# Spreading attention queries over edges as three bf16 parts instead of float32, in a graph kernel on one core

## What is computed

```python
q = (h @ Wq.T + bq)[dst]; k = (h @ Wk.T + bk)[src]; v = (h @ Wv.T + bv)[src]   # 8 heads of 16
alpha = jnp.sum(q * k, axis=-1) / 4
ex = jnp.exp(alpha - segment_max(alpha, dst)[dst])
out = segment_sum(ex / segment_sum(ex, dst)[dst] * v, dst)
x_r = h @ Ws.T + bs; h = gate(out, x_r) ...; layer norm; feed-forward          # 4 layers
msg = silu([x[src], x[dst], rbf(edge_len)] @ mw1 + mb1) @ mw2 + mb2             # message layer
agg = segment_sum(msg, dst) / count
```

## Time and profile before

| | |
|---|---|
| median of 3 runs | 7938.27 us (7920.73 to 7941.61) |
| the profiled execution's own time | 7866.28 us |
| its span in the trace | 7864.5 us |
| mean granted clock of TensorE | 0.685 of full |
| busy: PE, PEld, VectorE | 4591.8, 3687.8, 4054.1 us |
| busy: ScalarE, POOL | 2762.9, 3848.5 us |

### The profile page before, as it was taken

One profiled execution on the slowest core, in us unless ns is written; L12 is line 12 of the kernel. 1 busy time (PEld: TensorE's weight loads), 2 busy tenths in 40 slices (PEclk: granted clock), 3 DMA queues, 4 the chain that ended last, 5 costly groups with the idle time before them and its releaser, 6 DMA issues.

```text
span 7864.5 us, 105863 instructions
## 1 busy us (share of the span) xinstructions
PE 4591.8 (58%) x22799; PEld 3687.8 (47%) x22800; DVE 4054.1 (52%) x11127; ACT 2762.9 (35%) x6393; POOL 3848.5 (49%) x4061
## 2 busy tenths in 40 slices
PE   4555555655555556555555565555555655666666
PEld 2444444534444445344444453444444544555555
DVE  4555555645555556455555564555555653333334
ACT  1333333423333334233333342333333432333333
POOL 3555555335555553345555543455555425555553
PEclk6666666676666666766666667666666677878788
DMA  4222222122222222222222222222222211111111
GB/s 127 78 78 74 78 78 77 52 66 76 78 77 79 76 79 57 65 69 77 77 79 77 79 61 68 68 78 78 78 76 80 60 31 44 44 45 45 45 44 27
DMA packets 267185, 536.12 MB, mean 68 GB/s; under 512 B 116251, under 2 KB 148687, under 8 KB 266507
## 3 DMA queue, kind: packets, MB, share of 16 engines
q0 software_dynamic: 180992, 490.24, 23.2%
q1 hardware_dynamic: 78899, 35.89, 1.8%
q10 hardware_dynamic: 6936, 6.69, 0.3%
HBM read 512.41 MB, written 18.03 MB: 67 GB/s over the span
## 4 chain that ended last, share of the span: by engine, by line
PE 27%; another core or an unknown queue 25%; issue 20%; DVE 17%; ACT 5%; DVEq 4%; ACTq 1%; DMA 0%; SPq 0%; POOL 0%; POOLq 0%
PE bank L765 9%; PE bank L784 8%; DVE acc L1191 6%; PE bank L769 2%; PE bank L756 2%; ACT oh L549 2%; DVEq L330 2%; PE bank L805 2%; PE bank L833 1%; DVE alpha L1214 1%; DVEq L1191 1%; DVE slots L1283 1%; DVE oh L1175 1%; PE bank L937 1%
## 5 line engine op out<-in xcount | busy, mean ns | idle before, releaser
L504 POOL DMA_INDIRECT slots<-kv_table,idx x3224 | 3065.0, 951 | 3149.1 <-PE bank L784 1272.7
L784 PE MATMUL bank<-slots,oh 128*128 128x136 f32 (+1 forms) x8060 | 1598.6, 352 | 584.7 <-DVE acc L1191 502.7
L765 PE MATMUL bank<-qs,ohT 128*128 x8080 | 1676.3, 354 | 230.3 <-ACT ohT L540 132.0
L784 PEld LDWEIGHTS bank<-slots,oh 128*128 128x128 f32 x8060 | 1415.4, 253 | 716.9 <-DVE acc L1191 614.8
L765 PEld LDWEIGHTS bank<-qs,ohT 128*128 128x128 f32 x8080 | 1428.7, 256 | 450.4 <-issue 428.3
L1191 DVE TENSOR_TENSOR acc<-acc,bank 128x136 f32 (+1 forms) x4030 | 1173.6, 291 | 603.7 <-PE bank L784 166.4
L1208 DVE TENSOR_TENSOR slots<-slots,bank 128x512 f32<-128x512 f32 x808 | 552.3, 684 | 1312.1 <-remote 1294.4
L540 ACT ACTIVATE ohT<-bank,miss 128x512 f32<-128x512 f32 x1010 | 676.5, 683 | 1360.0 <-PE bank L756 1226.6
L504 POOL DMA_INDIRECT slots<-src_table,idx x806 | 760.8, 944 | 750.5 <-DMA idx<-src_e 233.6
L549 ACT ACTIVATE oh<-iota,rel_e 128x128 f32<-128x128 f32 x3168 | 962.9, 387 | 0.0
L797 PE MATMUL bank<-ident,alpha 128*128 128x128 f32 x204 | 93.7, 459 | 1459.5 <-DVE alpha L1214 1423.0
(11 more groups left out here) (255 smaller groups left out, 4032.7 us busy)
## 6 DMA issues: line engine op xcount, KB each, us to landing
slots<-kv_table,idx POOLq DMA_INDIRECT x3224
kv_table<-slots SPq DMA_DIRECT2D x20, 660.0 KB, 3.4
slots<-src_table,idx POOLq DMA_INDIRECT x806
resets<-flat_len ACTq DMA_DIRECT2D x51, 128.0 KB
idx<-src_e SPq DMA_DIRECT2D x255, 8.0 KB
terms<-flat_rel SPq DMA_DIRECT2D x255, 12.0 KB
resets<-flat_rst SPq DMA_DIRECT2D x2, 1551.0 KB
w<-in_w SPq DMA_DIRECT2D x8, 256.0 KB
```

Source lines behind the costliest of these rows:

```text
L504: pool.indirect_dma_start(slots[:, k, t, 0:width], None, table, bass.IndirectOffsetOnAxis(ap=idx[:, k, t:t + 1], axis=0))\
L765: mm = pe.matmul(o, ohT[:, j % 2, t, :], qs[:, blocks[j * G + t], 0:HID], start=True, stop=basis is None)
L784: mm = pe.matmul(bank[6 + part % 2][:, o:o + width], oh[:, k % 2, t, :], slots[:, k, t, HID:HID + width], start=True, stop=True)
```

## The change

Queries (and the destinations' part in the message pass) are kept as three bf16 numbers whose sum is their float32 value: the first two in the place in `qs` where the float32 value stood (`q_pair`), the third in a new tile `q_low`. `ohT` becomes bf16. Line 765 becomes three bf16 matmuls that add into the same PSUM place. VectorE makes the parts five blocks at a time (`in_parts`: a copy to bf16, a difference, a copy, a difference, over 5 x 128 columns). At a layer's start a block is therefore taken in two instructions, the query half into a float32 place in `oh`, the skip half into `qs`. A new semaphore `parts_done` holds PE back from the first spreading of a layer. The memory that software-made transfers use for their descriptors is set to 8192 bytes of a partition.

```diff
+        q_low = sb("q_low", [P, NB, HID], BF16)
+        q_pair = qs[:, :, :].bitcast(BF16)
-        ohT = sb("ohT", [P, 2, G, P])
+        ohT = sb("ohT", [P, 2, G, P], BF16)
+        whole = oh[:, 1, BW:2 * BW, :]
...
-                    mm = pe.matmul(o, ohT[:, j % 2, t, :], qs[:, blocks[j * G + t], 0:HID],
-                                   start=True, stop=basis is None)
+                    b = blocks[j * G + t]
+                    pe.matmul(o, ohT[:, j % 2, t, :], q_pair[:, b, 0:HID], start=True, stop=False)
+                    pe.matmul(o, ohT[:, j % 2, t, :], q_pair[:, b, HID:2 * HID], start=False, stop=False)
+                    mm = pe.matmul(o, ohT[:, j % 2, t, :], q_low[:, b, :], start=False, stop=basis is None)
...
+                pe.wait_ge(parts_done, START + NI * (l + 1))
...
+            pe.wait_ge(parts_done, START + NI * (L + 1))
...
+            def in_parts(first, end, rest, step):
+
+                step(dve.tensor_copy(q_pair[:, first:end, 0:HID], rest))
+                step(dve.tensor_tensor(rest, rest, q_pair[:, first:end, 0:HID], ALU.subtract))
+                step(dve.tensor_copy(q_pair[:, first:end, HID:2 * HID], rest))
+                return dve.tensor_tensor(q_low[:, first:end, :], rest, q_pair[:, first:end, HID:2 * HID], ALU.subtract)
...
-                    dve.tensor_tensor(qs[:, b, :], bank[6 + b % 2][:, 0:QS], vec_qs[:, :], ALU.add).then_inc(q_ev, 1)
+                    if b % BW == 0 and b > 0:
+                        dve.wait_ge(parts_done, START + NI * l + b // BW)
+                    dve.tensor_tensor(whole[:, b % BW, :], bank[6 + b % 2][:, 0:HID], vec_qs[:, 0:HID], ALU.add)
+                    dve.tensor_tensor(qs[:, b, HID:QS], bank[6 + b % 2][:, HID:QS], vec_qs[:, HID:QS], ALU.add).then_inc(q_ev, 1)
+                    if b % BW == BW - 1:
+                        dve.wait_ge(q_ev, START + NB * l + b + 1)
+                        in_parts(b - BW + 1, b + 1, whole, step).then_inc(parts_done, 1)
...
-                dve.tensor_tensor(qs[:, i * BW:i * BW + 4, 0:HID], bank[7][:, :].rearrange("p (b k) -> p b k", b=4),
+                dve.tensor_tensor(o_c[i][:, 0:4, :], bank[7][:, :].rearrange("p (b k) -> p b k", b=4),
                                   bc(bias, 4), ALU.add).then_inc(pair_q, 1)
-                dve.tensor_tensor(qs[:, i * BW + 4, 0:HID], bank[4][:, 0:HID], bias, ALU.add).then_inc(pair_q, 1)
+                dve.tensor_tensor(o_c[i][:, 4, :], bank[4][:, 0:HID], bias, ALU.add).then_inc(pair_q, 1)
+                dve.wait_ge(pair_q, START + 2 * i + 2)
+                in_parts(i * BW, (i + 1) * BW, o_c[i], step).then_inc(parts_done, 1)
...
-    nc = bacc.Bacc("TRN2", target_bir_lowering=False, num_devices=1)
+    nc = bacc.Bacc("TRN2", target_bir_lowering=False, num_devices=1, dynamic_dma_scratch_size=8192)
```

More of the change, by code:

```diff
@@ L270, in build_program @@
         rcol_done, fwd_one, bwd_one = sem("rcol_done"), sem("fwd_one"), sem("bwd_one")
+        parts_done = sem("parts_done")
         rows_turned, rows_copied, carry_set = sem("rows_turned"), sem("rows_copied"), sem("carry_set")
@@ L280, in build_program @@
         out_ready, out_sent = sem("out_ready"), sem("out_sent")
-        counted = [sums_ready, deviations_ready, x_sums, x_devs, in_ps, in_act, s_ps, q_ev, h_ev, f2_ps, wo_ps, wo_ev, x_new, x_ps, x_out, src_ps, dst_ps, r_ps, pair_q, pair_s, a_ev, a_ps, acc_done, part_ps, acc_scaled, acc_zero, act_ans, act_req,
+        counted = [parts_done, sums_ready, deviations_ready, x_sums, x_devs, in_ps, in_act, s_ps, q_ev, h_ev, f2_ps, wo_ps, wo_ev, x_new, x_ps, x_out, src_ps, dst_ps, r_ps, pair_q, pair_s, a_ev, a_ps, acc_done, part_ps, acc_scaled, acc_zero, act_ans, act_req,
                    alpha_done, alpha_turned, arg_done, b_done, bwd_one, bwd_two, carries_packed,
@@ L1467, in new_x, with destinations @@
                 dve.wait_ge(x_new, START + i + 1)
-            def destinations(i):
+            def destinations(i, step):
                 bias = vec1[:, VEC1["mb1"]:VEC1["mb1"] + HID]
                 dve.wait_ge(dst_ps, START + i + 1)
-                dve.tensor_tensor(qs[:, i * BW:i * BW + 4, 0:HID], bank[7][:, :].rearrange("p (b k) -> p b k", b=4),
+                dve.tensor_tensor(o_c[i][:, 0:4, :], bank[7][:, :].rearrange("p (b k) -> p b k", b=4),
                                   bc(bias, 4), ALU.add).then_inc(pair_q, 1)
-                dve.tensor_tensor(qs[:, i * BW + 4, 0:HID], bank[4][:, 0:HID], bias, ALU.add).then_inc(pair_q, 1)
+                dve.tensor_tensor(o_c[i][:, 4, :], bank[4][:, 0:HID], bias, ALU.add).then_inc(pair_q, 1)
+                dve.wait_ge(pair_q, START + 2 * i + 2)
+                in_parts(i * BW, (i + 1) * BW, o_c[i], step).then_inc(parts_done, 1)
             def finish_group(l, i, step, last):
@@ L1482, in finish_group @@
                 if i > 0:
-                    destinations(i - 1)
+                    destinations(i - 1, step)
             def layer(l, last):
@@ L1519, in layer @@
                 if last:
-                    destinations(NI - 1)
+                    destinations(NI - 1, step)
                 else:
@@ L1523, in layer @@
                 assert step.n == K_LAYER + (K_LAST if last else 0), step.n
-            K_BEGIN = 1 + NI
-            K_LAYER, K_LAST = 1 + 10 * NI, 6 * NI
+            K_BEGIN = 1 + 4 * NI
+            K_LAYER, K_LAST = 1 + 13 * NI, 9 * NI
             def take(k):
```

## The result

Sixteen timed executions of each kernel beside one another gave 7934.4 us for the kernel before (median) and 7977.0 for the changed one: ratio 1.006, 95% interval 1.0045 to 1.0076. The change makes the kernel 0.6% slower, 43 us. Forecast were 7879 us and a gain.

What follows compares the result with a forecast made beforehand. PE's signals, late while POOL issues gathers, and the engines' own part of each chunk were taken as the bound. Net 91 - 22 - 10 = 59 us off the profiled 7866.3, by share 7879 from the 7938.3 median; whole range 7715 to 8065.

Steps and rivals of the forecast that it cites:

- (1) Spreading: Query spreading in the edge loop: a group takes 1.28 us instead of 1.71, gaining 0.43 us a chunk, 81 us.
- rival B: Spreading gains nothing, because loads aren't hidden or PE's sequencer, computing an address per product, binds: 7970 us, chance 0.14.
- (6) The 8 KB: Smaller space for dynamic transfers: 0, since space isn't short; from above some 20 us at each of five starts.
- D: Rival: transfer space too small, so gather bursts at layer starts stop: 5 x 20 = +100 us, 7980; chance 0.05.
- Rival A: Edge loop: a shorter PE path makes POOL's two short gather runs join, lengthening chunks: 8060 us, chance 0.24.
- (1), messages: Spreading in the message stage, whose product waits for the same late signal: gain 0, at most 22 us.
- (2) Making the parts: Four more VectorE operations per five blocks, mostly hidden in layer-start waits: costs 22 us, 68 if later waits lack room.
- (3): Making parts before the messages, five more groups, the last exposed: costs 10 us, from 3 to 17.
- (4): New waits, VectorE for its own last take and PE for all parts before a layer's first spreading: 0.
- (5): ScalarE writes its one-hots as bf16, with the same columns: 0.

Runs made afterwards that it cites:

- eight addresses: Changed kernel with 16 KB for dynamic transfers, third product repeating the middle part: against before, 1.0031 to 1.0034 where signals are prompt, 1.0104 where late.

## Why the prediction was wrong, point by point

**(1) Spreading.** This is the step that failed first. The path was right, and so was the price of a product; the bound was not. Twelve bf16 products take 1.27 us at half clock where PE's sequencer keeps up; in the changed kernel it doesn't, and the group on the path takes 1.73 (median), against 1.86 before: 0.13 us gained, not 0.43. The adding group behind it then takes 0.16 more: its first weight load starts with its first product, where that of before started 0.21 us ahead, behind the spreading products. That was rival B's mechanism (the sequencer computes an address per product), to which I gave 0.14. The trace of before had what was needed: four register instructions a group in PE's queue, 0.125 us apart, hidden behind eight products. I counted products and never the instructions of the queue that feeds them. That the chunks with eight addresses are 27.0 us long, as forecast, is in part luck: their group is 0.59 us shorter than the 1.86 of before, not 0.43 (the sum took 1.71 for it), and their adding group gives 0.11 back. In the full-clock part too the sequencer sets the group: the fourth of a chunk, from its start to the next line, has 1.05 us in the changed kernel (median), 0.89 before, 0.78 with eight addresses and 0.67 with none. The 1.05 that the prediction read for before counts the end of its last product. The prediction's end value for that case, 1.3, was too high, its other end, 0.66, holds where no address is computed.

Rival B gave 7970 us, near the 7977 measured, but by other terms: 32 us for the making of parts, nothing for the restart and nothing lost in the messages. The nearness is luck.

The rule cited there, of the Trainium skill, "TensorE: Matmul & The Clock Gate", section "Back-to-back issue gap", about 81 ns for a load and matmul pair with 128 columns, does not agree with these traces: 55 ns in the rows above when PE's queue is filled, 125 ns when each product needs an address.

The chunks without gathers, for which I had 10 us of gain, gained nothing. The scans of the last chunks of layer 0, the two of before that enclose the 1520.01 and 1538.72 of the earlier trace rows, and then those of the changed kernel:

```profile
...
1500.89 0.48 DVE L1264 TENSOR_TENSOR_SCAN fwd<-resets,icol,bank 128x128 f32<-128x128 f32 x1 [1.06 <-issue]
...
1556.54 0.48 DVE L1264 TENSOR_TENSOR_SCAN fwd<-resets,icol,bank 128x128 f32<-128x128 bf16 x1 [0.88 <-issue]
...
```

```profile
...
1523.39 0.48 DVE L1272 TENSOR_TENSOR_SCAN fwd<-resets,icol,bank 128x128 f32<-128x128 f32 x1 [1.06 <-issue]
...
1541.99 0.48 DVE L1272 TENSOR_TENSOR_SCAN fwd<-resets,icol,bank 128x128 f32<-128x128 bf16 x1 [1.13 <-issue]
...
1561.58 0.48 DVE L1272 TENSOR_TENSOR_SCAN fwd<-resets,icol,bank 128x128 f32<-128x128 bf16 x1 [0.89 <-issue]
...
1578.86 0.48 DVE L1272 TENSOR_TENSOR_SCAN fwd<-resets,icol,bank 128x128 f32<-128x128 bf16 x1 [0.88 <-issue]
...
```

The changed kernel's are 18.6, 19.6 and 17.3 us apart; before has 19.1, 18.7 and 17.8 at this place. 55.5 against 55.6.

**(6) The 8 KB,** priced at 0, with D's 100 us for bursts that stop. No burst of 64 gathers stops: with the 8 KB alone they take 78.9 to 79.0 us in layers 1 to 3, as before (78.7 to 78.8), and in the changed kernel 79.9 to 81.9. D was the wrong mechanism in the right place. This is the second step that failed: what came is 0.20 us at every restart in the loop. On the path of a separate chunk it takes back the 0.13: from the adding group's start to the next run of eight it is 3.15 us instead of 2.79, 0.20 of it the restart and 0.16 the adding group. So the path loses 0.23 us where 0.43 were forecast as a gain; the separate chunks are 27.62 us long (27.66 in the second trace of the changed kernel), before 27.45. Over 188 chunks that is some 30 to 40 us, an estimate from these medians. The 8 KB alone pushed nearly all chunks into the joined form and cost 1.68%. With both parts of the change in place 33 and 41 of 176 chunks are joined, about as in before, so the parts keep them apart; that they do it by the shorter group is my reading, no run shows it. The change as a whole is thus a loss of 1.7% that the parts bring down to 0.4% (both on the one chip).

**Rival A** had a form that does decide much of the time, but in the changed kernel it did not grow: 33 and 41 joined chunks, 38 before. With the 8 KB alone a later third run joins nearly all. With the shorter path there are more too (58 instead of 38), though between two chips, so the cause that A named is argued and not shown. A's own price had a slip: 180 less 40 are 140 chunks, not 150, half of them 168 us and not 180.

**(1), messages.** Forecast 0 to 22 us of gain; measured 31 us of loss, chunks of 27.56 us instead of 26.82, and of 26.81 when that stage alone went back to float32. The granted clock there fell from 0.80 to 0.73, and the last product of a chunk starts on VectorE 24.0 us into it instead of 23.1, although PE ends the fourth group of spreading 1.5 us earlier (at 17.1 instead of 18.6). The signal's arrival isn't set by its sending there. What sets it is open, and with it why this term became a loss. On prompt chips this stage has no loss: its gathers take 1006 to 1009 us in all traces, with the parts and without.

**(2) Making the parts.** Right: 0.82 us an operation, forecast 0.86. In layers 1 to 3 it hides in the waits, as said: the gaps between layers are 2.7 us shorter in sum. In layer 0 the first scan with the carries (line 1272, 1264 before) comes 10.5 us later. Forecast were 22 us, 10 for layer 0 and 12 for the rest: the 10 came, of the 12 the gaps show nothing. **(3)** 12.7 us, forecast 10, at most 17. On prompt chips, where little else differs, the kernel with eight addresses shows both: 19 us. **(4), (5)** nothing seen, as forecast.

**What stays open.** Where the 70 us lie by which the first profile of before is under its median, and so the true sizes in the table; what the parts with all twelve addresses cost without the longer restart where signals are late; why a PE signal comes late on some chips; why the 8 KB lengthen the restart.

## What to carry to other kernels

Before one instruction is split into several with computed operands, count the register instructions of the engine's queue per group and their spacing: here 4 at 0.125 us were free, 8 nearly so, and 12 were the bound. A size that only configures a transfer queue is a change of its own; run it alone. And in a loop that locks to the phase of another engine's bursts, a term of 0.2 us can do more than its sum says (1.7% here, with longer chunks in the layers and shorter ones in the messages), so sum the terms only within one form of the chunk and price the change of form by itself.

## What the runs showed of the hardware that I had not expected

- The same kernel takes 5660 to 5669 us on four chips, and 7850 to 7950 in the three other groups of runs. On the former hardly a PE signal is late (10 to 30 signals later than 2 us in the whole kernel, against more than a thousand in the trace of before above), and POOL's 1.25 us a gather sets the time.
- POOL's first gather after a wait in the loop starts 0.73 us after the wait instruction with 16 KB for dynamic transfers and with 12032 bytes (one wait in each of two traces), 0.93 with 8 KB; inside a run nothing changes.
- Two products with the same computed operand share one address computation; load and product pairs of 128 bf16 columns follow at 0.107 us at 1.2 GHz and 0.055 at 2.4 GHz when nothing else holds PE.
- With a third of the spreading products taken away the granted clock was 0.704 instead of 0.744, and the kernel was slower.
